# A GRU with attention and a gated second recurrence on one core: the gated part from ten items behind the GRU to six, attention scores per pair of items

## The reference

```python
# GRU over the 50 steps
z = sigmoid(x Wz + h Uz + b); r = sigmoid(x Wr + h Ur + b)
hc = tanh(x Wh + b0 + r * (h Uh + b1));  h = z*h + (1-z)*hc
# attention score of each step, from h and the last input "news"
emb = concat(h, news-h, news, h*news)
a = relu(emb W1 + b1); a = relu(a W2 + b2); s = sigmoid(a W3 + b3)
# gated recurrence over the same steps, reads h and s
u = s*sigmoid(h Wu + g Uu + bu); r = sigmoid(h Wr + g Ur + br)
c = tanh(h Wc + bc + r * (g Uc)); g = (1-u)*g + u*c
# head on concat(g, news): batch norm, 256, 128, 1
```

## Time and profile before

| | |
|---|---|
| median of 3 runs | 1911.28 us (1911.26 to 1912.22) |
| profiled execution, its own time | 1911.32 us |
| its span (first to last instruction) | 1909.5 us |
| PE busy | 1893.0 us, 17389 records |
| DVE, ACT, POOL busy | 1541.1, 1443.9, 1636.4 us |
| granted TensorE clock | 1.000 |

### The profile page before, as it was taken

The page is one execution under the profiler, slowest core; times in us unless marked ns, Lnnn a source line. Parts: engine busy times, 40 slices in busy tenths (PEclk is TensorE's granted clock), DMA queues, the critical chain, the costliest instruction groups (busy, mean ns, idle before and its releaser), DMA issues. The chain is left out here.

```text
span 1909.5 us, 46007 instructions
## 1 busy us (share of the span) xinstructions
PE 1893.0 (99%) x17389; PEld 986.4 (52%) x17389; DVE 1541.1 (81%) x2401; ACT 1443.9 (76%) x2470; POOL 1636.4 (86%) x1391
## 2 busy tenths in 40 slices
PE   8999999999999999999999999999999999999998
PEld 4455555555555555555555555555555555555554
DVE  7899988778787877888787778878887877888776
ACT  7778777777777777777777777777777777777775
POOL 7789988888888888888888888888888888888873
PEclk9999999999999999999999999999999999999999
DMA  4211211121121112111211211121112112111100
GB/s 126 79 51 52 73 51 51 51 73 51 51 72 55 51 53 73 51 51 51 73 51 51 68 57 50 56 74 51 51 51 73 51 51 64 60 51 54 65 24 23
DMA packets 50259, 110.65 MB, mean 58 GB/s; under 512 B 16948, under 2 KB 17332, under 8 KB 43704
## 3 DMA queue, kind: packets, MB, share of 16 engines
q1 hardware_dynamic: 49960, 107.99, 17.9%
q10 hardware_dynamic: 144, 0.26, 0.1%
HBM read 107.39 MB, written 0.42 MB: 56 GB/s over the span
## 5 line engine op out<-in xcount | busy, mean ns | idle before, releaser
L1161 PE MATMUL ps<-h_hi,w_hi 128*64 128x512 f16 x1384 | 524.9, 379 | 6.5 <-DVE t L918 3.0
L1162 PE MATMUL ps<-h_hi,w_hi 128*64 128x512 f16 x1384 | 525.0, 379 | 0.0
L1162 PE MATMUL ps<-h_lo,w_hi 128*64 128x512 f16 x1384 | 524.5, 379 | 0.0
L1162 PE MATMUL ps<-h_hi,w_lo 128*64 128x512 f16 x1384 | 524.5, 379 | 0.0
L1161 PE MATMUL ps<-h_lo,w_hi 128*64 128x512 f16 x1384 | 524.5, 379 | 0.0
L1161 PE MATMUL ps<-h_hi,w_lo 128*64 128x512 f16 x1384 | 524.5, 379 | 0.0
L341 POOL TENSOR_TENSOR hn_lo<-hn,hn_hi 128x512 f16<-128x512 f32 x200 | 232.8, 1164 | 143.5 <-ACT hn_hi L483 143.5
L335 POOL TENSOR_TENSOR hn<-h,news 128x512 f32<-128x512 f32 x200 | 255.9, 1280 | 72.0 <-DVE h L1038 71.4
L628 ACT ACTIVATE ps<-gt,p_rest 128x512 f32<-128x512 f32 x185 | 127.7, 690 | 200.8 <-DVE gt L1035 200.8
L354 POOL TENSOR_TENSOR x_lo<-x,x_hi 128x512 f16<-128x512 f32 x196 | 228.8, 1168 | 17.6 <-ACT x_hi L503 13.4
L414 POOL TENSOR_TENSOR d<-h,hc 128x512 f32<-128x512 f32 x186 | 238.3, 1281 | 0.0
(11 more groups left out here) (182 smaller groups left out, 6843.8 us busy)
## 6 DMA issues: line engine op xcount, KB each, us to landing
score<-score_rows SPq DMA_DIRECT2D x50, 1024.0 KB, 4.6
x<-in_xs SPq DMA_DIRECT2D x199, 256.0 KB, 3.1
part_up<-part SPq DMA_DIRECT2D x100, 4.0 KB, 1.8
score_rows<-s_col SPq DMA_DIRECT2D x100, 4.0 KB, 1.4
news<-in_xs SPq DMA_DIRECT2D x4, 256.0 KB, 4.8
p_rest<-in_pack_rest SPq DMA_DIRECT2D x1, 776.0 KB, 6.9
p_att<-in_pack_att SPq DMA_DIRECT2D x1, 290.0 KB, 4.6
x<-in_xs ACTq DMA_DIRECT2D x1, 256.0 KB, 4.0
```

The lines of the kernel that those rows point to most:

```text
L1161: m.matmul(ps[0:H, bank, :], weights[:, 0:H], moving, start=start, stop=stop)
L1162: return m.matmul(ps[H:P, bank, :], weights[:, H:P], moving, start=start, stop=stop)
```

## The change

LAG goes from 10 to 6, so that the gated part of an item is done six slots behind its GRU, and the number of slots that have only the gated part goes from ten to six. The second attention layer is done for one pair of items in every second slot, behind R on PE, with `relu_2` and the new `weigh_2` on ACT, `sum_2` on DVE in the same slot and `total_of` and `scores_of` in the next; the DMA queue lifts and spreads per pair (`score` has two buffers of two items), and its loop is written out. `weigh_2` multiplies by W3 itself where `sign_2` multiplied by its sign, and it writes its output in another order, so that it reads PSUM with a stride of 16 elements and `sum_2` reads without one. `prepare_att_2` goes. The first slots have a new order on ACT (`first_slot`), POOL and DVE; the small operations on the batch norm (`bn_...`) are spread over slots 16 to 38, one in a slot; the last two pairs have their own places in `late`.

```diff
--- before.py
+++ after.py
...
-    LAG = 10
+    LAG = 6
     HIST = 3 * NC
-    LOOP_LO = 7 * NC
+    LOOP_LO = 10 * NC
...
-    TILED = 5
-    FOLDED = TILED + 3
+    TILED = 4
+    FOLDED = TILED + 1
...
-        return low % NC == TILED % NC and has(low - TILED)
...
+        return low % 2 == TILED % 2 and low > TILED and has(low - TILED)
...
-        return low % NC == FOLDED % NC and has(low - FOLDED)
...
+        return low % 2 == FOLDED % 2 and low > FOLDED and has(low - FOLDED)
...
-            def lift_partials(done):
-                sp.wait_ge(part_ready, done)
+            def lift_partials(pair):
+                p = pair % 2
+                sp.wait_ge(part_ready, 2 * pair + 2)
                 for k in range(2):
-                    sp.dma_start(part_up[k * H:k * H + Q, :, :], part[k * H + Q:(k + 1) * H, :, :]).then_inc(part_landed, 16)
-            def spread_scores(group, buffer):
-                if not isinstance(group, int) or group > 0:
-                    sp.wait_ge(score_landed, 16 * group)
-                sp.wait_ge(s_ready, NC * group + NC)
-                rows = score_rows.rearrange("(g k) (b j) -> k b g j", k=2, b=Q)
+                    sp.dma_start(part_up[k * H:k * H + Q, p, :], part[k * H + Q:(k + 1) * H, p, :]).then_inc(part_landed, 16)
+            def spread_scores(pair):
+                p = pair % 2
+                sp.wait_ge(s_ready, 2 * pair + 2)
+                if pair >= 2:
+                    sp.wait_ge(score_landed, 16 * (pair - 1))
                 for k in range(2):
-                    sp.dma_start(rows[k], s_col[k * H:k * H + Q, :, :]).then_inc(rows_stored, 16)
-                if not isinstance(group, int) or group >= HIST // NC:
-                    sp.wait_ge(gus_ready, NC * group - HIST + NC)
-                sp.wait_ge(rows_stored, 32 * group + 32)
-                sp.dma_start(score[:, buffer, :, :], score_rows.partition_broadcast(P)).then_inc(score_landed, 16)
-            def scores_between(step, c, buffer):
-                known = isinstance(step, int)
-                if c == 0 and (not known or step >= 3):
-                    spread_scores(step - 3, buffer)
-                if c == 2 and (not known or step >= 2):
-                    lift_partials(NC * step - NC)
+                    row = score_rows[2 * p + k].rearrange("(b j) -> b j", b=Q)
+                    sp.dma_start(row, s_col[k * H:k * H + Q, p, :]).then_inc(rows_stored, 16)
+                if pair >= 2:
+                    sp.wait_ge(gus_ready, 2 * pair - 2)
+                sp.wait_ge(rows_stored, 32 * pair + 32)
+                sp.dma_start(score[:, p, :, :], score_rows[2 * p:2 * p + 2].partition_broadcast(P)).then_inc(score_landed, 16)
+            def scores_between(step, c):
+                pair = 2 * step - 5 + (c + 1) // 2
+                if 0 <= pair < ITEMS // 2:
+                    if c % 2 == 0:
+                        spread_scores(pair)
+                    else:
+                        lift_partials(pair)
...
+            for c in range(3):
+                load_step(2, c)
+            lift_partials(0)
+            spread_scores(0)
+            load_step(2, 3)
+            lift_partials(1)
...
                 g.tensor_tensor(lo, p_state[:, :], hi, ALU.subtract).then_inc(state_split, 1)
             def early(low):
-                if low + 2 >= NC + 2:
-                    if low == NC:
-                        pool.wait_ge(xlo_ready, NC + 2)
+                state_news(low - 1, low)
+                if has(low - LAG - 1):
+                    gated_share(low - LAG - 1, low - LAG, 16 * ((low - LAG - 1) // 2 + 1))
+                state_low(low - 1, low)
+                state_news_low(low - 1, low)
+                if low + 2 > NC:
+                    if low + 2 == NC + 1:
+                        pool.wait_ge(xlo_ready, NC + 1)
                     input_low(low + 2, low + 3)
-                if has(low - LAG - 1):
-                    gated_share(low - LAG - 1, low - LAG, 16)
-                if has(low - 1):
...
             state_news_high(1, 2)
             news_part(0)
             news_part(1)
-            second_high(1)
             news_part(2)
-            state_news_high(2, 3)
             relu_1_high(0, 1)
-            second_high(2)
...
-            def relu_2(p, count):
-                act.wait_ge(a2_pe[p], count)
-                a.activation(ps[:, B_PAIR[p], :], ps[:, B_PAIR[p], :], ACT.Relu, bias=b_att2[:, 0:1],
-                             scale=w3_col[:, 3:4]).then_inc(a2p_ready[p], NC)
-            def sign_2(p, count):
-                act.wait_ge(a2p_ready[p], count)
-                if not isinstance(count, int) or count > NC:
-                    act.wait_ge(part_ready, count - NC)
-                a.activation(a2[:, p, :], ps[:, B_PAIR[p], :], ACT.Identity, scale=w3_col[:, 2:3]).then_inc(a2_ready[p], NC)
...
+            def relu_2(count):
+                act.wait_ge(a2_pe, count)
+                a.activation(ps[:, B_PAIR, :], ps[:, B_PAIR, :], ACT.Relu,
+                             bias=p_att[:, PACK_ATT["b2"]]).then_inc(a2p_ready, 2)
+            def weigh_2(p, count):
+                act.wait_ge(a2p_ready, count)
+                if not isinstance(count, int) or count > 4:
+                    act.wait_ge(part_ready, count - 4)
+                a.activation(a2[:, p, :].rearrange("p (j b) -> p j b", b=Q),
+                             ps[:, B_PAIR, :].rearrange("p (b j) -> p j b", b=Q), ACT.Identity,
+                             scale=p_att[:, PACK_ATT["w3"]]).then_inc(a2_ready, 2)
...
+            def first_slot():
+                reset_gate(NC)
+                state_news_high(2, 3)
+                second_high(1)
+                state_high(3, 4)
+                relu_1_high(1, 2)
+                candidate(NC)
+                update_gate(NC)
+                news_part(3)
+                state_news_high(3, 4)
+                second_high(2)
+                split_gated_high(0)
+                relu_1_high(2, 3)
+                input_high(NC + 3, 32, NC)
...
+                if pairs_of(low):
+                    relu_2(at(3))
+                    weigh_2((low - TILED) // 2 % 2, at(3))
                 if folds_of(low):
-                    scores_of(folded(s0 + off))
+                    scores_of((low - FOLDED) // 2 % 2, at(4))
                 if has(low - LAG):
...
-            def prepare_att_2():
-                w3 = p_att[:, PACK_ATT["w3"]]
-                v.tensor_scalar(w3_col[:, 0:1], w3, 0.0, None, ALU.is_gt).then_inc(prep, 1)
-                v.tensor_scalar(w3_col[:, 1:2], w3, 0.0, None, ALU.is_lt).then_inc(prep, 1)
-                v.scalar_tensor_tensor(out=w3_col[:, 3:4], in0=w3, scalar=-1.0, in1=w3,
-                                       op0=ALU.mult, op1=ALU.max).then_inc(prep, 1)
-                dve.wait_ge(prep, 5)
-                v.tensor_tensor(w3_col[:, 2:3], w3_col[:, 0:1], w3_col[:, 1:2], ALU.subtract).then_inc(prep, 1)
-                v.tensor_tensor(b_att2[:, :], p_att[:, PACK_ATT["b2"]], w3_col[:, 3:4], ALU.mult).then_inc(prep, 1)
...
-                v.tensor_reduce(part[:, p, :], a2[:, p, :].rearrange("p (b j) -> p j b", b=Q), AX.X, ALU.add,
...
+                v.tensor_reduce(part[:, p, :], a2[:, p, :].rearrange("p (j b) -> p j b", b=Q), AX.X, ALU.add,
...
             def early(low):
                 k = low % 2
-                if folds_of(low):
-                    total_of(folded(low))
-                if pairs_of(low - 1):
...
+                if low == TILED + 1:
+                    sum_2(0, 2)
                 attention_1_low(item, item + 1)
+                if pairs_of(low):
+                    sum_2((low - TILED) // 2 % 2, low - 2)
+                if folds_of(low):
+                    total_of((low - FOLDED) // 2 % 2, low - 3)
...
+                    split_gated_low(0)
                     attention_1_low(2, 3)
-                if low == SPLIT_X:
-                    split_gated_low(0)
+                if low == FOLDED:
+                    total_of(0, 2)
...
                 def late(lag):
                     return s0 + (off - lag + 1 - NC)
-                if folds_of(low):
-                    total_of(folded(s0 + off))
-                if pairs_of(low - 1):
-                    sum_2(0, paired(s0 + (off - 1)))
                 if has(low - 2):
                     attention_1_news(low - 2, at(2))
                 if has(low - LAG - 1):
                     gated_difference(low - LAG - 1, at(LAG + 1))
-                if pairs_of(low - 1):
-                    sum_2(1, paired(s0 + (off - 1)))
                 if has(low):
                     k = low % 2
                     dve.wait_ge(hh_pe, late(0))
                     dve.wait_ge(r_ready, at(0))
                     v.scalar_tensor_tensor(out=t[:, k, :], in0=ps[:, B_HH, :], scalar=b_hs,
                                            in1=r[:, k, :], op0=ALU.add, op1=ALU.mult).then_inc(t1_ready, 1)
+                if folds_of(low):
```

(28 more changed lines are left out.)

261 lines of the change are left out of this document (115 added, 146 removed).

## The result

The changed kernel takes **1902.61 us** (median of 5 runs, 1902.53 to 1902.91), the kernel before 1911.75 (5 runs, 1911.26 to 1912.41). The ratio is 0.9952, with a 95% interval of 0.9941 to 0.9963. The profiled span went from 1909.5 to 1900.9 us, 8.6 less.

A forecast was written before the change was run, and what follows sets the result against it. The prediction took the kernel to be bound by its number of matmuls, with gains only at the two ends: 1911.3 - 6.1 (start) - 0 (middle) - 2.0 (tail) = 1903.2 us, between 1900.5 and 1908.1.

The forecast's parts named there:

- the start: From 20 to 110 us: 11.6 us missing, 5.5 kept as stall, gain 6.1 us, between 3.2 and 7.8.
- What bounds: Whole kernel: bound by the number of matmuls, which stays; only the two ends can gain, 15.3 us at most.
- Slot 4: At the start: at least 2.8 us leave the head of DVE's attention chain, so this slot's stalls go.
- Slots 5 to 9: At the start, DVE's work against PE's: slot 5 keeps 0.9 to 2.0 us, slot 6 nothing, 7 to 9 2.9 to 5.1.
- waits for L906: Sign in the profile after: PE waits for this DVE line in slots 7 to 10.
- Slot 10: At the start, where the other order begins: stall of nothing at one end, 1.3 us at the other.
- It comes about because six GRU-only slots become two.: Reason for the start's 6.1 us: slots 5 to 10 become 5 and 6, filled by gated products arriving earlier.
- The end that the prediction drew from the rule: DVE and POOL exclude each other on SBUF, so `total_of` inside the slot keeps 8.4 us of stall; by median row 3.8.
- Middle: Loop between the ends: cost 0; ACT's `gu` ends at 6.48 us, Z starts at 7.12, margin 0.64.
- `weigh_2` breaks the margin: Slower rival ahead of Z: strided PSUM read on ACT costs from +0.64 us; at +0.8, 1918 us; slower chance 0.15.
- Tail: From 1840 us: 3.7 us to win, 1.3 kept for local waits, last scores charged 0.4; gain 2.0, between 0 and 3.
- Batch norm, transfers: In the middle: small DVE operations up to about 1 us each, one per slot, and score transfers covered: cost 0.

The follow-up runs named there:

- run 4: Kernel before, with the third attention weight's preparation moved behind slot 4 and x_lo of item 5 given to POOL: 1912.38 us, ratio 1.0004.
- run 5: Kernel before, with only the new order of the first slots on ACT and POOL, x_lo of item 5 on POOL, preparation left in place: 1910.52 us.
- run 6: Changed kernel, with the five preparation operations put back on DVE at their old place: 1904.11 us.
- run 2: Changed kernel, with all gated operations of slots 7 to 9 ahead of t2 on DVE and gus ahead of the state's news on POOL: 1901.23 us.
- run 10: Changed kernel, with LAG 8 instead of 6: 1902.82 us, ratio 0.9952.
- run 7: Changed kernel, with extra ACT copies of 128x512 behind the pair's weighing in each even slot: four copies 2039.33 us, one copy 1903.10 us.
- run 3: Changed kernel, with the last pair's total of scores issued on DVE behind the gated state of slot 203 instead of behind gt2: 1901.49 us.
- run 9: Changed kernel, with the weighed products written contiguously and summed with a stride, as before: 1902.90 us.
- run 1: Changed kernel, with the gated difference on DVE right behind t1 in slots 7 to 9 instead of behind t2: 1901.23 us, ratio 0.9946.

## Why the prediction came out, and where it didn't

The time, 1903.2, was 0.6 us from the measured one. Two terms were off in opposite directions: the start gave 7.3 us where 6.1 were forecast, the end 1.2 where 2.0 were.

**What bounds.** Right. PE was full from slot 12 to slot 199, and everything moved at the ends.

**Slot 4.** The step "`prepare_att_2` and the second `x_lo` go from DVE [...] so at least 2.8 us leave the head of that chain" names one owner of several. The stalls did go (0.31 us of gaps left to 37 us). But run 4 takes the same operations off the head of the chain, and slot 4 stalls on for 2.2 us, with ACT's and POOL's order the old one. The order alone leaves 2.6 us of gaps (run 5), and the preparation put back into the new order brings 1.6 (run 6). So both were needed, and the prediction, which mentioned the order, gave it no share. How much the preparation alone held in the old order stays open.

**Slots 5 to 9.** Comparing DVE's work with PE's priced slots 7 to 9 at 2.9 to 5.1 us; gaps there are 1.22, 1.14 and 1.14 us, 3.5. Run 2, with DVE busy throughout, bears the mechanism out for 2.45 of them, less than the 2.9 of the lower end; the other 1.05 was order, which the prediction didn't price here. It was to show as waits for L906; it showed as waits for `g` L833, since that is DVE's later result in the same slot. Slot 5 was to keep 0.9 to 2.0 and kept nothing: the sum took 0.70 us instead of 1.05, and the total 0.17. This is most of the 1.2 us by which the start was undersold. Slot 10 kept nothing, its lower end; 0.24 us stand in slot 11, ahead of GU.

**"It comes about because six GRU-only slots become two."** Not borne out. With lag 8 there are four, and the time is the same (run 10). Run 5 shows that with lag 10 and scores in fours the later slots keep their 7 to 8.5 us. Which of the two, the step from 10 to 8 or the scores by pairs, took about half of that away stays open; no run had lag 10 with scores by pairs. The trace of the kernel before points to the scores. Its two longest gaps there, 1.50 us at 53.90 and 1.34 at 80.53, 2.8 of 6.9 us, stand behind a total of 1.25 us at the head of the slot, ahead of the `t` that PE waits for (DVE, POOL, PE of the kernel before; the second case is in the earlier trace rows):

```profile
51.93 1.25 DVE L813 TENSOR_TENSOR total<-part,part_up 128x32 f32<-128x32 f32 x1
53.10 0.74 DVE L918 SCALAR_TENSOR_TENSOR t<-ps,p_gru,r 128x512 f32<-128x512 f32 x1
...
51.54 1.59 POOL L335 TENSOR_TENSOR hn<-h,news 128x512 f32<-128x512 f32 x1
...
80.53 0.40 PE L1161 MATMUL ps<-h_hi,w_hi 128*64 128x512 f16 x1 [1.18 <-DVE t L918]
```

The change puts the total behind `t`, so a long one no longer stands ahead of it. That this is what the later slots gained is read from the timelines; no run tests it.

**The total and the port.** The end that the prediction drew from the rule was too dark, and the median row was right: 166 ns. It called the change worse off for having the total inside the slot; the place at the slot's head was the costly one, as the rows above show. The rule itself holds where the two meet (run 2; the Trainium skill, "SBUF — State Buffer", "Who interferes with whom": the trace agrees, 1.13 us beside POOL, 0.17 without). It says what a meeting costs, and only the timeline says how often they meet.

**Middle.** Zero, right, and for the reason given. The margin of 0.64 us came out at 0.64 (run 7). The rival "`weigh_2` breaks the margin" needed 0.64 us more; the strided read of PSUM took 0.687 us, as the plain one. Its price law, 95 times what goes over, gives (2.08 - 0.64) · 95 = 136.8 us for run 7, and 136.7 were measured. Here my later theory, that ACT's idle time would cushion it, was the wrong one: I had overlooked that the two gates share a bank.

**Tail.** The mechanism was right, two terms were mis-sized. The last scores were charged 0.4 us, "2 at the worst", and cost 1.4, of which 1.2 come back with the total two operations earlier (run 3). And the 3.7 us to be won were too many: the window of the earlier trace rows holds some f32 matmuls of the head, which take twice as long, and the gaps of the kernel before at the end are 3.1 us. Against that the other local waits were 0.7 us, below the 1.3 kept for them. That 1903.2 came so close is in part luck: the start gave 1.2 us more than forecast and the end 0.8 less.

**Batch norm, transfers.** Nothing of either shows as a wait of PE in the loop.

## What to carry to other kernels

A stall can have several engines behind it, each late by itself. Moving work from one of them to another that stands in the same chain gained nothing (run 4), and work taken away was worth 1.5 us where the others were no longer late (run 6). Judge slack by the next writer of the buffer, not by an engine's idle time: 24% idle on ACT did not cover 2 us in front of a shared PSUM bank, and the 0.64 us read from two timelines was right. Where the very last item has a long chain of transfers, its place in program order counts: two operations earlier were worth 1.1 us, while in the loop 35 us of extra DVE work (run 9) and 49 us of extra ACT work (one copy, run 7) showed nothing.

## What the runs showed that I had not expected

Up to the first attention product the same instructions run at two speeds. The weight preparation of 128x128 on DVE takes 0.28 us in one execution and 1.36 us in another. In the slow one POOL began 0.11 us ahead of it (changed kernel, DVE, then POOL):

```profile
11.59 1.36 DVE L782 TENSOR_TENSOR p_att<-p_att 128x128 f32<-128x128 f32 x1
16.51 1.43 DVE L790 TENSOR_TENSOR w_lo<-p_att,w_hi 128x320 f16<-128x320 f32 x1
...
11.48 1.33 POOL L325 TENSOR_TENSOR hn<-h,news 128x512 f32<-128x512 f32 x1
```

and in run 1, where DVE came first, 0.03 us ahead of POOL:

```profile
11.19 0.28 DVE L782 TENSOR_TENSOR p_att<-p_att 128x128 f32<-128x128 f32 x1
15.74 1.05 DVE L790 TENSOR_TENSOR w_lo<-p_att,w_hi 128x320 f16<-128x320 f32 x1
```

In the slow case L782 ends 0.14 us behind POOL's `hn`, and slot 4 of run 1 began 0.9 us earlier than the changed kernel's. Over the fourteen traces the first attention product begins between 17.1 and 19.4 us. This, and loads that land some tenths of a microsecond apart, is the likely source of the spread of 1 to 2 us between runs; that it is the whole of it was only argued, and run 4's profile has 1.4 us of a low clock besides.

A transposing sum over 512 f32 columns takes 1.06 us when it reads SBUF with a stride and 0.70 when it reads in order, while ACT's read of PSUM with the same stride of 16 elements costs nothing extra (0.687 us, as the plain one).
